# Second cross attention: softmax denominators taken as rows on four column tiles and turned into columns, with two later steps moved back by two tiles

## The reference

```python
def _L1_xattn_ref(x, context, mask, Wq, Wkv, Wout, b_out):
    HEADS = 16
    DIM_HEAD = 64
    SCALE = DIM_HEAD ** (-0.5)
    B, Nq, _ = x.shape
    Nkv = context.shape[1]
    q = x @ Wq.T
    kv = context @ Wkv.T
    k, v = jnp.split(kv, 2, axis=-1)
    ...
    sim = jnp.einsum('bhid,bhjd->bhij', q, k) * SCALE
    max_neg = -jnp.finfo(sim.dtype).max
    sim = jnp.where(mask[:, None, None, :], sim, max_neg)
    attn = jax.nn.softmax(sim, axis=-1)
    out = jnp.einsum('bhij,bhjd->bhid', attn, v)
    out = out.transpose(0, 2, 1, 3).reshape(B, Nq, HEADS * DIM_HEAD)
    return out @ Wout.T + b_out
```

## Time and profile before

| what | value |
|---|---|
| median of 3 runs | 3620.03 us (3610.92 to 3620.97) |
| the profiled execution: its own time, its span | 3617.19 us, 3615.4 us |
| TensorE products busy | 3324.3 us, 92% of the span |
| TensorE weight loads busy | 1948.3 us, 54% |
| VectorE busy | 2414.3 us, 67% |
| ScalarE busy | 1943.2 us, 54% |
| GpSimd busy | 1549.1 us, 43% |
| costliest group: line 1929, the mix, 1664 products | 804.8 us, mean 604 ns |

### The profile page before, as it was taken

The page is one execution under the profiler, slowest core; times in us unless marked ns, Lnnn a source line. Parts: engine busy times, 40 slices in busy tenths (PEclk is TensorE's granted clock), DMA queues, the critical chain, the costliest instruction groups (busy, mean ns, idle before and its releaser), DMA issues. The chain is left out here.

```text
span 3615.4 us, 67907 instructions
## 1 busy us (share of the span) xinstructions
PE 3324.3 (92%) x26493; PEld 1948.3 (54%) x26619; DVE 2414.3 (67%) x5544; ACT 1943.2 (54%) x2669; POOL 1549.1 (43%) x1219
## 2 busy tenths in 40 slices
PE   6889999999996679599999999999999998979998
PEld 4646666666664467355555545555554554655555
DVE  5757777777774443477777777777777776563333
ACT  4436566666664313466666666666666664432222
POOL 2034333333330000277777777777777776210000
PEclk9979999999997669699999999999999998979999
DMA  1033333333320000201111111101111100010000
GB/s 56 12 71 76 74 76 75 79 71 75 77 62 1 1 25 1 70 20 36 37 37 37 37 37 37 33 23 37 37 37 37 37 28 1 1 73 1 1 1 12
DMA packets 90496, 139.23 MB, mean 39 GB/s; under 512 B 14464, under 2 KB 67776, under 8 KB 89408
## 3 DMA queue, kind: packets, MB, share of 16 engines
q1 hardware_dynamic: 90176, 134.87, 13.8%
HBM read 94.41 MB, written 1.05 MB: 26 GB/s over the span
## 5 line engine op out<-in xcount | busy, mean ns | idle before, releaser
L2111 ACT ACTIVATE arena<-banks,arena 128x512 f32<-128x512 f32 x832 | 560.9, 687 | 477.4 <-PE banks L1904 476.6
L1929 PE MATMUL banks<-arena 128*128 128x512 f32 x1664 | 804.8, 604 | 3.0 <-ACT arena L2118 3.0
L1863 POOL TENSOR_TENSOR arena<-arena 128x1024 f32<-128x1024 f32 x256 | 604.1, 2360 | 166.5 <-ACT arena L2118 165.6
L1110 DVE TENSOR_REDUCE arena<-banks 128x1 f32<-128x512 f32 (+1 forms) x896 | 529.3, 627 | 187.0 <-PE banks L995 181.7
L2013 DVE TENSOR_TENSOR banks<-arena,banks 128x512 f32<-128x512 f32 x640 | 444.4, 694 | 243.5 <-ACT arena L2111 223.5
L1207 ACT ACTIVATE arena<-banks 128x1024 f32<-128x1024 f32 (+1 forms) x448 | 425.1, 964 | 315.9 <-PE banks L1016 313.0
L2030 DVE TENSOR_TENSOR arena<-arena,banks 128x1024 f32<-128x1024 f32 (+1 forms) x448 | 507.1, 1133 | 1.5 <-PE banks L1919 1.0
L2118 ACT ACTIVATE arena<-arena 128x1024 f32<-128x1024 f32 (+1 forms) x448 | 443.0, 989 | 11.6 <-DVE arena L2030 11.4
L1929 PEld LDWEIGHTS banks<-arena 128*128 128x128 f32 x1664 | 290.1, 190 | 223.0 <-issue 202.5
L1904 PE MATMUL banks<-arena 128*128 128x512 bf16 x831 | 314.7, 379 | 2.6
L1903 PE MATMUL banks<-arena 128*128 128x512 bf16 x785 | 298.5, 380 | 4.3 <-issue 0.2
(11 more groups left out here) (346 smaller groups left out, 5280.4 us busy)
## 6 DMA issues: line engine op xcount, KB each, us to landing
arena<-in_ctxT SPq DMA_DIRECT2D x64, 800.5 KB, 5.7
arena<-arena SPq DMA_DIRECT2D x768, 50.0 KB, 2.2
arena<-in_ctx SPq DMA_DIRECT2D x32, 768.0 KB
arena<-in_m2w SPq DMA_DIRECT2D x3, 2048.0 KB, 12.2
arena<-in_xw SPq DMA_DIRECT2D x1, 2048.0 KB, 7.7
weights<-in_weights SPq DMA_DIRECT2D x1, 1918.0 KB, 7.5
arena<-in_ctx SPq DMA_DIRECT2D x32, 32.5 KB
arena<-in_m1w SPq DMA_DIRECT2D x1, 1024.0 KB, 6.3
```

The costliest lines, as they stand in the source:

```text
L1110: eng.tensor_reduce(o, s, AX, ALU.max).then_inc(a_max, 1)
L1863: eng.tensor_tensor(part, part, tiles, ALU.add).then_inc(sums, 1)
L1929: eng.matmul(c.ps[:, R_MIX + v % 2, :], ctxn[:, b, kt * D:(kt + 1) * D], st[:, v % 2, kt, :], start=kt == 0, stop=kt == KT - 1).then_inc(m ...
L2111: eng.activation(st[:, v % 2, kt, :], c.ps[:, n % SB, :], ACT.Identity, bias=hide[:, kt, v // 2:v // 2 + 1])\
```

## The change

The four denominator products change sides: a 32-column piece of ones is the weights, the 128 columns of `total` stream, and each of the four writes its own 32 partitions of the bank (the same row 32 times). VectorE takes the reciprocal of that whole 128x128 block (`reciprocal`). A new product, `turn_recips`, multiplies it with a new constant `quad`, 128x4, that picks one row of each 32, which gives a 128x4 block of columns; VectorE copies it (`keep_recips`). `turn_recips` stands at kt 3, the projection moves from kt 3 to kt 5, and the peaks with `maxima` from kt 5 to kt 7. `spread_shift` stays at kt 8.

```diff
--- before.py
+++ after.py
@@ -74,7 +74,7 @@
            ("den_a", L), ("den_b", L),
            ("causal", L), ("rot", P), ("cos", L), ("sin", L), ("cosq", L), ("sinq", L), ("dist", L), ("head4", 4),
            ("off2", 2),
-           ("twice", 2 * P), ("minus", P)]
+           ("twice", 2 * P), ("minus", P), ("quad", 4)]
 C_AT, C_N = layout(C_ITEMS)
 
 
@@ -124,6 +124,7 @@
     t["minus"] = -np.eye(P)
     row = np.arange(2 * P)[None]
     t["twice"] = 1.0 * (p[:, None] == row // P * L + row % L)
+    t["quad"] = (p[:, None] == HR * np.arange(4)[None])
     t["dist"] = np.clip(np.arange(L)[None] - (p % L)[:, None], 0, None)
     return np.concatenate([np.asarray(t[n], np.float32).reshape(P, w) for n, w in C_ITEMS], 1)
 
@@ -1795,7 +1796,7 @@
     mh, ml = k.bf16(TU), k.bf16(TU)
     unit = k.bf16(P)
     part, total = k.f32(2, QU), k.f32(QU)
-    rden = k.f32(2, TU)
+    rden, rrow = k.f32(2, TU), k.f32(P)
     u = k.f32(2, QU)
     acc = k.f32(2, D)
     first_acc = k.f32(D)
@@ -1811,7 +1812,8 @@
     p_ps, mx_made, mx_high, mx_low, m_ps = (sem(f"max_{n}") for n in ("turned", "made", "high", "low", "spread"))
     shifted, exps, sums = sem("shifted"), sem("probs"), sem("probs_summed")
     mixed, u_made = sem("mixed"), sem("mix_copied")
-    d_ps, recips, y_ps, y_added = sem("den_psum"), sem("recips"), sem("y_psum"), sem("y_added")
+    d_ps, row_recips, r_ps, recips = sem("den_psum"), sem("row_recips"), sem("recips_psum"), sem("recips")
+    y_ps, y_added = sem("y_psum"), sem("y_added")
     bias_ready, f_ps, out_made = sem("bias_ready"), sem("out_psum"), sem("out_made")
     R_MAX, R_SHIFT, R_MIX, R_SMALL = 3, 4, 5, 7
     SPLIT = 4
@@ -1930,11 +1932,17 @@
                        start=kt == 0, stop=kt == KT - 1).then_inc(mixed, 1)
 
         def denominators(v):
-            take_small((recips, v + 1))
+            take_small((row_recips, v + 1))
             eng.wait_ge(sums, (v + 1) * NP)
             for t in range(TU):
-                mm = eng.matmul(c.ps[:, R_SMALL, t:t + 1], total[:, t * P:(t + 1) * P], c.one[:], start=True, stop=True)
+                mm = eng.matmul(c.ps[HR * t:HR * t + HR, R_SMALL, 0:P], c.one[:].to_broadcast([P, HR]), total[:, t * P:(t + 1) * P],
+                                start=True, stop=True)
             mm.then_inc(d_ps, 1)
+
+        def turn_recips(v):
+            take_small((recips, v + 1))
+            eng.wait_ge(row_recips, v + 1)
+            eng.matmul(c.ps[:, R_SMALL, 0:TU], rrow, c.C("quad"), start=True, stop=True).then_inc(r_ps, 1)
 
         def project(v):
             take_small((y_added, TU * (v + 1)))
@@ -1977,8 +1985,10 @@
             if kt == 1 and v > 0:
                 denominators(v - 1)
             if kt == 3 and v > 0:
+                turn_recips(v - 1)
+            if kt == 5 and v > 0:
                 project(v - 1)
-            if kt == 5 and v + 1 < UNITS:
+            if kt == 7 and v + 1 < UNITS:
                 turn_peaks(v + 1)
             if kt == 8 and v + 1 < UNITS:
                 spread_shift(v + 1)
@@ -2032,8 +2042,13 @@
 
         def reciprocal(v):
             eng.wait_ge(d_ps, v + 1)
+            wait_if(eng, r_ps, v)
+            eng.reciprocal(rrow, c.ps[:, R_SMALL, 0:P]).then_inc(row_recips, 1)
+
+        def keep_recips(v):
+            eng.wait_ge(r_ps, v + 1)
             wait_if(eng, y_added, TU * (v - 1))
-            eng.reciprocal(rden[:, v % 2, :], c.ps[:, R_SMALL, 0:TU]).then_inc(recips, 1)
+            eng.tensor_copy(rden[:, v % 2, :], c.ps[:, R_SMALL, 0:TU]).then_inc(recips, 1)
 
         def project(v):
             bt, b = v // 2, v // 2 % 2
@@ -2088,7 +2103,9 @@
                 running_max(n + LEAD)
             if kt == 1 and v > 0:
                 reciprocal(v - 1)
-            if kt == 5 and v + 1 < UNITS:
+            if kt == 3 and v > 0:
+                keep_recips(v - 1)
+            if kt == 7 and v + 1 < UNITS:
                 maxima(v + 1)
             if (v % 4, kt) in QUERIES and v // 4 + 1 < PAIRS:
                 queries(v // 4 + 1, QUERIES[v % 4, kt])
@@ -2097,7 +2114,7 @@
             a = n + SUB_AHEAD
             if a < TILES and a % KT % 2 == 0:
                 shift(a // KT, a % KT // 2)
-            if kt == 3 and v > 0:
+            if kt == 5 and v > 0:
                 project(v - 1)
```

## The result

The changed kernel takes 3636.7 us (median of all 6 runs) against 3619.0 for the kernel before (6 runs): the ratio is 1.0052, 95% interval 1.0034 to 1.0070. **It is 0.5% slower, where I had forecast 9 us less.** One of the six runs, of 6904.7 us, stands by itself and is not in the ratio; the median of the other five is 3634.1 us.

The account below looks back on a forecast made before the run. TensorE was taken as the bound, at 23.99 us per unit. Denominators and turning (-0.32 + 0.26) and the lost wait (-0.12) give -0.18 us x 62; with -0.1 and end + 1.1, -10.2 us: 3610 us, range 3602 to 3620.

Parts of the forecast that it names:

- What bounds the kernel: Whole stage: TensorE sets the unit's time, busy 95.53 of 95.96 us over four units.
- the 0.12 us at the transposes: TensorE before the peaks' transposes: 0.12 us lost per unit waiting for VectorE's additions, to go to 0.
- Denominators, turning product: TensorE, per unit: denominators cost 0.57 us instead of 0.89; the added product turning the reciprocals costs 0.26.
- rows 6: Profile rows before the change: four products on 32-column tiles start within 0.06 us, taken to show the tiles run at once.
- the 0.93 us: VectorE's added work per unit, 0.77 for the reciprocal and 0.16 for the copy, to be covered by two idle stretches.
- Projection two tiles later: Projection and peaks moved: VectorE's additions end 4.20 us after the scores, signal included, against TensorE's 4.24, so no wait.
- the 1.73: Term in VectorE's chain between the running maximum at 0.91 us after the scores' end and the last 1.51.
- passed by nothing: Claim that nothing moves past GpSimd, SP's queue and its DMAs; the constants only grow by 4 columns, once.
- The spreading: Shift's spreading on TensorE: comes some 3.5 us after the transposes, VectorE's chain takes 2.81, so 0.7 to spare.
- End of the stage: Last unit, denominators to projection: 2.35 us instead of 1.30, so + 1.1 us, once.
- The sum: Whole kernel: -0.18 us per unit x 62 = -11.2, two last units -0.1, end + 1.1, in all -10.2 us.
- VectorE's longer work: Rival: VectorE's added work reaches the waits at the transposes, where the margin is 0.04 us; 3632 or about 3620; chance 0.08.

Follow-up runs that it names:

- a1_split_45: Changed kernel with GpSimd's splitting of the next context moved, in odd units, from behind additions 2 and 4 to 4 and 5: 3603.6 us, ratio to before 0.9971.
- a3_copy_then_recip: Changed kernel with VectorE copying the 128x128 rows and taking the reciprocal last, of the turned 128x4: ratio to before 1.0056.
- a2_one_input: Changed kernel whose running maximum at tile 1 reads tile 1 alone, so tile 0 is missing from the peaks: ratio to before 0.9975.
- b1_split_34: Kernel before with GpSimd's splitting in odd units moved from behind additions 2 and 4 to 3 and 4: ratio 0.9998.
- b4_split_23: Kernel before with GpSimd's splitting in odd units moved from behind additions 2 and 4 to 2 and 3: ratio 1.0004.
- a5_shift_first: a1_split_45 with, on VectorE at tile 7, the last tile's shift and the maxima ahead of the running maximum: ratio to before 0.9981.
- b2_moves_only: Kernel before with only the projection moved from tile 3 to 5 and the peaks with maxima from 5 to 7: ratio 1.0069.
- a1_again: a1_split_45 measured once more, on the same chip as a repeat of a5_shift_first: 3608.1 us, ratio to before 0.9976.

## Why the prediction was wrong

*What bounds the kernel: right.* TensorE, and the 0.12 us at the transposes hidden behind a modelled end. It did go where nothing else came between, in all units of a1_split_45.

*Denominators, turning product: right in kind, a little high.* 0.57 was 0.55, 0.26 was 0.22. The four column tiles run at once, as rows 6 said: the eight passes (2206.63) are followed 0.35 us later by the mix (2206.98), where one after another they would stream 0.86. The Trainium skill ("TensorE: Matmul & The Clock Gate", Part 3, on packing small matmuls) says that a weight load overlaps running products only where the row groups differ; these tiles share all rows, so the measurement is against it and decides.

*VectorE: right.* The reciprocal takes 0.95, the turning product never waited for it, and the 0.93 us were absorbed (a3_copy_then_recip).

*Projection two tiles later: this is the step that failed.* "The other starts when ScalarE's copy is there: ... 0.91 after the scores' end. Then 0.91 + 1.73 + 1.51 = 4.15." The start was right; the 1.73 held a running maximum of 0.70, measured at places where one of its inputs lay in PSUM or GpSimd was quiet. The one without a predecessor is the only one with both inputs in SBUF, and at its new time GpSimd is adding in every second unit. It takes 1.69 there, the additions end at 5.16 and not 4.15 after the scores (2242.59 against 2237.43), against the 4.24 that TensorE has. With it falls the sentence that GpSimd is "passed by nothing": no instruction moves past another in GpSimd's list, but the two engines' times moved against each other. The rows that I needed were in the trace of before. GpSimd's timeline and VectorE's, in the unit whose denominators are at 2226.13:

```profile
2232.61 2.35 POOL L1863 TENSOR_TENSOR arena<-arena 128x1024 f32<-128x1024 f32 x1
```

```profile
2235.19 0.70 DVE L2013 TENSOR_TENSOR banks<-arena 128x512 f32<-128x512 f32 x1 [0.85 <-ACT arena L2111]
```

GpSimd's addition ends at 2234.96, VectorE's operation begins 0.23 us later. I moved it 1.4 us forward against the denominators and looked at ScalarE and TensorE alone. The collision itself was there to see as well, once, ahead of the first denominators. GpSimd and VectorE in the kernel before:

```profile
1537.98 2.35 POOL L1863 TENSOR_TENSOR arena<-arena 128x1024 f32<-128x1024 f32 x1 [0.75 <-ACT arena L2118]
```

```profile
1540.00 0.89 DVE L2013 TENSOR_TENSOR banks<-arena 128x512 f32<-128x512 f32 x1 [1.19 <-ACT arena L2111]
```

It is the one operation of the 64 that takes 0.89 us and not 0.70, and it begins 0.33 us before GpSimd's addition ends: 0.19 added, with the same 0.14 between.

The Trainium skill ("SBUF — State Buffer", section "Who interferes with whom") says that a VectorE instruction with two SBUF inputs contends with a GpSimd instruction that reads SBUF, that the order of issue decides who blocks, and, of VectorE's modes that use both ports, that the one that issues first has the shared pair for its whole instruction while the other is blocked fully. a1_split_45, a2_one_input, b1_split_34 and b4_split_23 agree with it, in both directions, and this operation behaves like those modes, with the 0.14 us noted above. I had not read it beside this trace.

*The spreading: wrong in small.* I gave it 0.7 us to spare and looked at the maxima only, and for them 0.7 was right. Its other wait, for the shift of the unit's last tile, which now comes behind the maxima, ends 0.07 too late in the short units; a5_shift_first moved it.

*End of the stage:* 1.1 was 0.9.

*The sum.* -0.18 us per unit is what the undisturbed units show. 30 disturbed units at 0.91 more give 27 us, which turns the forecast's -10.2 into +17. Measured in the traces are +15.1 in the stage and +0.9 at its end, 16 in all; a good part of the difference is that the three last stretches are 1.5 us shorter together, where I had about -0.5. In b2_moves_only the last two of them are 1.0 shorter (17.34 and 14.60 for 17.68 and 15.26), so most of it goes with the moves; no run shows the cause. The chances had the slower side at 0.12, for VectorE's longer work, a mechanism that did not occur; its price was worked out by the same margin of 0.04 us at the transposes, and that margin was real.

## What to carry to other kernels

Before an operation is moved in time, list its inputs: where two lie in SBUF, put GpSimd's timeline beside the old and the new time, not only the engines that it waits for. The sign in a profile is one form of a line whose mean length grows, with no idle time to show for it; look at the lengths in single units. A schedule by hand can be repaired on the other engine: two of GpSimd's four splits behind later additions, where nobody waits for them, turned 0.5% slower into 0.2 to 0.3% faster.

## What the runs showed that I had not expected

- The block between VectorE and GpSimd goes by who begins first: with 0.03 us of lead VectorE kept its 0.70 and GpSimd's 0.92 became 1.44; with GpSimd 0.27 ahead VectorE's 0.70 became 1.06. GpSimd released it 0.13 to 0.14 us before the end of its row in all four cases, if the blocked operation is taken to need the 0.70 that it takes alone. In a1_split_45 VectorE begins some 0.12 before the end of GpSimd's row (2230.37 against 2228.13 + 2.36 = 2230.49) and takes 0.70: it escapes by about 0.02 us.
- Units repeat to 0.02 us over the whole stage, while whole runs of one program scatter by 15 us. The unit's length told apart what the medians could not. One unit in the kernels with the splitting moved is an exception: 23.88 us in a1_split_45 and 23.90 in a1_again in place of 23.53, with TensorE late at the spreading (2142.02) behind 0.46 us in which VectorE stands idle in the middle of the maxima. The changed kernel has the same idle time (2148.0), in a long unit. Why is not known; a2_one_input has it too, so it is not the collision.
